# Two DMAs where there was one for the stacked heads, and a denser order for normalising the next batch, in an attention stage between two expert layers

## The reference

```python
x = x + 0.5 * ffn(layernorm(x))        # top 2 of 8 experts, silu(gate) * up, down
x = x + attn(layernorm(x))             # 16 heads of 16
x = x + 0.5 * ffn(layernorm(x))

# attn
q = x @ W_q ; k = x @ W_k ; v = x @ W_v
latent = (k + v) @ W_down_kv           # 64 wide
k_rec, v_rec = latent @ W_up_k, latent @ W_up_v
scores = (q k_rec^T) / 16 * exp(-0.01 |i - j|)
out = softmax(scores) @ v_rec @ W_o
```

## Time and profile before

| what | value |
|---|---|
| median of three runs | 6439.68 us (6439.29 to 6446.07) |
| the profiled execution | 6439.29 us, its span 6437.5 us |
| attention stage in the span | about 1110 to 5320 us |
| one batch of it, from batch 3 on | about 252.9 us (64 steps) |
| mean granted TensorE clock over the span | 0.946 |

### The profile page before, as it was taken

How to read it: one execution, slowest core, us unless ns; L and a number is a source line. 1 busy time by engine, 2 the same in 40 slices (tenths; PEclk the granted TensorE clock), 3 DMA queues, 4 the chain that set the end, 5 groups by cost and what they waited for, 6 DMA issues and landing times.

```text
span 6437.5 us, 111424 instructions
## 1 busy us (share of the span) xinstructions
PE 5494.3 (85%) x35660; PEld 3210.9 (50%) x35660; DVE 4607.0 (72%) x14349; ACT 3194.0 (50%) x4421; POOL 2850.2 (44%) x2837
## 2 busy tenths in 40 slices
PE   4459998379999999999999999999999993999771
PEld 4448887134444444444444444444444442888561
DVE  6556565268888888888888888888888883555453
ACT  1124443146666665666666666656666662444220
POOL 5630000653655646646546556466474332000445
PEclk9999999589999999999999999999999996999885
DMA  4423333344544544544445444445444432333556
GB/s 150 149 98 105 105 105 110 98 95 86 123 100 105 121 103 111 122 100 118 112 97 124 99 107 120 103 109 122 99 112 99 87 66 89 100 105 109 167 187 188
DMA packets 531513, 725.27 MB, mean 113 GB/s; under 512 B 79491, under 2 KB 447237, under 8 KB 530949
## 3 DMA queue, kind: packets, MB, share of 16 engines
q1 hardware_dynamic: 481796, 583.86, 37.7%
q0 software_dynamic: 49152, 134.28, 6.5%
HBM read 424.53 MB, written 293.34 MB: 112 GB/s over the span
## 4 chain that ended last, share of the span: by engine, by line
PE 59%; POOL 16%; DVE 10%; issue 9%; another core or an unknown queue 2%; ACT 2%; DMA 2%; SPq 1%; POOLq 0%; ACTq 0%; DVEq 0%
PE psum L1205 12%; PE psum L1055 11%; PE psum L374 11%; PE psum L1064 7%; PE psum L391 5%; DVE at_mx L1317 4%; PE psum L1068 2%; POOL at_xT L1440 2%; POOL at_XR L1471 2%; POOL at_Sd L1531 2%; PE psum L1112 2%; PE psum L363 2%; PE psum L382 2%; POOL at_XR L1449 2%
## 5 line engine op out<-in xcount | busy, mean ns | idle before, releaser
L1265 ACT ACTIVATE at_P<-psum 128x1024 f32<-128x1024 f32 x2048 | 2034.7, 1023 | 1317.0 <-PE psum L1068 1252.6
L1317 DVE TENSOR_REDUCE at_mx<-psum 128x4 f32<-128x512 f32 x3584 | 2229.1, 682 | 432.2 <-PE psum L1055 380.0
L1055 PE MATMUL psum<-at_kst,at_qst 96*128 96x128 bf16 (+3 forms) x7168 | 1611.2, 295 | 186.3 <-DVE at_mx L1317 124.8
L1064 PE MATMUL psum<-at_qst,at_kst 99*128 99x512 bf16 (+3 forms) x5120 | 1467.6, 320 | 7.2 <-ACT at_P L1265 7.1
L1055 PEld LDWEIGHTS psum<-at_kst,at_qst 96*128 96x128 bf16 x7168 | 598.5, 98 | 1491.5 <-DVE at_mx L1317 609.0
L1205 PE MATMUL psum<-at_P,at_V 128*17 128x512 f32 x8192 | 1099.3, 608 | 0.0
L1531 POOL TENSOR_TENSOR at_Sd<-at_Sd,at_m 128x1024 f32<-128x1024 f32 x256 | 484.4, 1898 | 943.5 <-DVE at_m L1326 941.7
L669 POOL DMA_INDIRECT m2Y<-ys,m2yi x256 | 243.5, 951 | 797.3 <-issue 626.3
L1068 PE MATMUL psum<-at_ident,at_Sd 128*128 128x128 f32 x2048 | 565.3, 276 | 0.0
L1064 PEld LDWEIGHTS psum<-at_qst,at_kst 99*128 99x128 bf16 x5120 | 493.7, 99 | 143.1 <-ACT at_P L1265 18.2
L1312 DVE CUSTOM_DVE_ANT_0 at_Sd<-psum,at_Dm 128x128 f32<-128x128 f32 x2048 | 443.2, 286 | 87.1 <-PE psum L1055 87.0
(11 more groups left out here) (246 smaller groups left out, 7950.6 us busy)
## 6 DMA issues: line engine op xcount, KB each, us to landing
parts<-at_pt SPq DMA_DIRECT2D x768, 128.0 KB
at_qst<-parts SPq DMA_DIRECT2D x768, 128.0 KB
at_kst<-parts SPq DMA_DIRECT2D x128, 384.0 KB
m2X<-xs SPq DMA_DIRECT2D x272, 128.0 KB, 2.0
ys<-m2X SPq DMA_DIRECT2D x272, 128.0 KB
m1X<-xs SPq DMA_DIRECT2D x264, 128.0 KB, 2.0
ys<-m1X SPq DMA_DIRECT2D x264, 128.0 KB
at_kst<-parts SPq DMA_DIRECT2D x128, 256.0 KB
```

The lines of the kernel that those rows point to most:

```text
L1055: ins = e.matmul(bank[z % 3][:, col - 512 * u:col - 512 * u + ln], self.qst[0:96, s, side, 128 * t:128 * t + 128], self.kst[0:96, s, 1 - s ...
L1064: e.matmul(slot[a % 2][:, q0:q0 + ln], self.kst[0:99, s, side, 128 * kb:128 * kb + 128], self.qst[0:99, s, 1 - side, q0:q0 + ln], start=Tr ...
L1265: e.activation(self.P[:, i % NP, :], slot[a % 2], ACT.Exp).then_inc(self.taken.sem, 1)
L1317: e.tensor_reduce(self.mx[:, p % 2, hh, 8 * o + 4 * u:8 * o + 4 * u + 4], of, op=ALU.max, axis=AX.X).then_inc(self.s_read.sem, 1)
```

## The change

The stack of a pair is issued head by head, so it takes 18 DMAs instead of 9, of half the size each; the semaphore counts follow (144 becomes 288). In `gather_order` the statistics are done two to a slot, `var` shares the slot of the last two, and the eight `center` are done in two slots instead of four, with no empty slot behind them. In `unit_order` the `send` of a projection comes right in the slot after its second `rest`, instead of in the next projection's.

```diff
-        self.stacked = sig.ring("a_stacked", [144 * n for n in shares_of(NPAIR, NS)])
+        self.stacked = sig.ring("a_stacked", [288 * n for n in shares_of(NPAIR, NS)])
...
         for t in range(8):
-            yield from (("stats", b, t), None)
+            yield ("stats", b, t)
+            if t % 2 and t < 7:
+                yield None
         yield from (("var", b), None, ("newton", b), None)
         for t in range(8):
             yield ("center", b, t)
-            if t % 2:
+            if t == 3:
                 yield None
         yield None
...
         for i in range(8):
-            yield from (("project", b, i), None, ("cast", b, i, 0), None, ("rest", b, i, 0))
-            if i:
-                yield ("send", b, i - 1)
-            yield from (None, None, ("cast", b, i, 1), None, ("rest", b, i, 1), None)
+            yield from (("project", b, i), None, ("cast", b, i, 0), None, ("rest", b, i, 0), None, None,
+                        ("cast", b, i, 1), None, ("rest", b, i, 1), None, ("send", b, i))
         for t2 in range(4):
-            yield ("values", b, t2)
-            if t2 == 2:
-                yield ("send", b, 7)
-            yield None
+            yield from (("values", b, t2), None)
...
-                    w.wait_ge(*self.stacked[s].at(144 * len(range(s, 8 * (b - 1), NS))))
+                    w.wait_ge(*self.stacked[s].at(288 * len(range(s, 8 * (b - 1), NS))))
...
-                h = 2 * (p % 8)
-                qd, kd = self.qst[:, 2 * s:2 * s + 2], self.kst[:, 2 * s:2 * s + 2]
-                for c, (r0, r1) in enumerate(((0, 3), (3, 5), (5, 6))):
-                    for r in range(r0, r1):
-                        e.dma_start(qd[16 * r:16 * r + 16], src[0, h:h + 2, c].rearrange("h d v t -> d h v t")).then_inc(done, 16)
-                for r0, n in ((0, 3), (48, 2), (80, 1)):
-                    e.dma_start(kd[r0:r0 + 16 * n], src[1, h:h + 2, 0:n].rearrange("h c d v t -> (c d) h v t")).then_inc(done, 16)
+                for hh in range(2):
+                    h = 2 * (p % 8) + hh
+                    qd, kd = self.qst[:, 2 * s + hh], self.kst[:, 2 * s + hh]
+                    for c, (r0, r1) in enumerate(((0, 3), (3, 5), (5, 6))):
+                        for r in range(r0, r1):
+                            e.dma_start(qd[16 * r:16 * r + 16], src[0, h, c]).then_inc(done, 16)
+                    e.dma_start(kd[0:48], src[1, h].rearrange("c d v t -> (c d) v t")).then_inc(done, 16)
+                    e.dma_start(kd[48:80], src[1, h, 0:2].rearrange("c d v t -> (c d) v t")).then_inc(done, 16)
+                    e.dma_start(kd[80:96], src[1, h, 0]).then_inc(done, 16)
...
-            w.wait_ge(*self.stacked[n // 2 % NS].at(144 * (n // 2 // NS + 1)))
+            w.wait_ge(*self.stacked[n // 2 % NS].at(288 * (n // 2 // NS + 1)))
```

## The result

The changed kernel takes 6646.19 us (median of 4 runs, 6639.33 to 6653.74) against 6442.88 us (4 runs) for the kernel before: a ratio of 1.0314, 95% interval 1.0297 to 1.0332. The forecast was slower, +150 us to 6589 with a range up to 6645. The measured change is +203, and the time lies 1 us above that range: the sign and the main cause hold, and one term is missing.

A forecast was written before the change was run, and what follows sets the result against it. PE and DVE were taken to run in lockstep over three banks, PE a little ahead. Denser gather 140, batches 0 to 2 5 + 3, first stack 2, earlier send 0: 150 on 6439.3, so 6589 us; 8-in-10 range 6495 to 6645.

The forecast's parts named there:

- the stop at the turn: PE at a batch's first turn transpose: stands 8.9 us for GpSimd's last center, against 0.7 before, 8.2 more.
- part 1: Denser gather order in the attention stage: 10.8 us per batch, 140 us over 13 batches.
- GpSimd's chain: GpSimd's own work from newton to the last center in a batch: 22.5 us.
- The clock term: PE at half clock behind the stop at the turn: +3.0 us for each batch.
- The crowding of DVE: Stats moved into steps 410 to 413, where DVE is the slower engine: +0.8 us a batch.
- The bounds between the halves: Denser gather order: bounds of 7 to 13 us a batch for the whole, no figure for stats or center alone.
- Batches 0 to 2: Gather of the first batches: nothing in batch 0, +5 us in batch 1, +3 in batch 2.
- the first stacks: At the start, where PE waits for the first stack issued as 18 DMAs: +2 us (0 to 4).
- The stacks: 18 DMAs for a stack on SP: transfers stay slower than 8.6 us of issues; steady stage pays nothing.
- the rival of late stacks: Fixed cost per DMA uses up the stacks' margin, so scores wait: about 6700 us, chance 0.09.
- The earlier send: Send two steps sooner on SP: may put msend off some 4 us, with at least 9 to spare: 0.
- part 4: The send issued two steps sooner on SP's queue: 0 us (0 to +15).

The follow-up runs named there:

- e2: Kernel before with only the denser gather order (stats in pairs, center in two slots, no empty slot behind): 6372.5 us, ratio 1.0223.
- e5: Changed kernel with 60 identity transposes on PE ahead of its wait at the first turn of batches 3 to 15: 6396.9 us, ratio 1.0258.
- e7: Kernel before with only the stats two to a slot and var with the last two: 6271.0 us, ratio 1.0059.
- e6: Kernel before with only the eight center in two slots and no empty slot behind them: 6376.1 us, ratio 1.0225.
- e1: Kernel before with only the stack issued head by head, 18 DMAs for 9: 6232.4 us, ratio 0.9996.
- e3: Kernel before with only the send moved right behind its second rest: 6299.0 us, ratio 1.0101.
- e8: Kernel before with the send one slot behind the next project, so behind msend on SP's queue: 6241.1 us, ratio 1.0005.
- e11: Kernel before with one more empty slot ahead of the turns and the stats begun one slot later: 6375.0 us, ratio 0.9893.

## Why the prediction was right in its direction and short by 53 us

- **Slower, by the stop at the turn** (part 1): right, nearly to the figure. GpSimd's chain 22.5 us forecast, 22.3 measured; the stop 8.9 and 8.05; the gain in a batch 10.8 and 10.4 (e2); the part as a whole 140 and 137. The clock term of 3.0 us is borne out by e5 with some 3 to 4, in the changed kernel. That the sum came out so near is in part luck, as the next point shows.
- **The crowding of DVE** (+0.8 a batch): too small. e7 shows 2.1, since the short stops behind DVE also pull the clock down. In the sum of part 1 this was made up by a stop 0.8 us shorter and by what came back elsewhere: in e2 PE's busy time grows by only 1.6 us a batch for crowding and stop together, and in e7 by 2.0 for the crowding alone.
- **The bounds between the halves**: the sum did not say what each half would do, and e6 shows that center in two slots is enough for all of it.
- **Batches 0 to 2** (+8) and the first stacks (+2): 3.4 us measured up to batch 3.
- **The stacks** (0 in the steady stage): right, and the rival of late stacks wrong (e1). The reason given, that the DMA engines are slower than 18 issues, was wrong: with smaller DMAs they got faster and had room while the issues went on. That the end came out nearly the same (11.3 us against 10.7) was luck.
- **The earlier send** (part 4: 0, at most +15): this is the step that failed. It said that msend may be put off by some 4 us and has at least 9 to spare. It is put off by 9.2, as the six issues (3.65 us) and the wait for a late rest (5.5 us) both count, and then its halves lie 2.8 us further apart (4.2 for 1.4): 12.0 in all. Of the 9.0 us between the last issue and PE in the kernel before, some 1.3 are the landing (3028.10 to 3029.41 in the changed kernel), so an estimate of what was to spare is 7.7, and the 4.3 that are missing are about PE's stop of 4.03. The 6.4 us at most of the earlier trace rows were waits of sends that came three steps after their rest; in the changed order the send comes one step after it and SP meets the rest itself, which on GpSimd stands behind r_center and gathers. It happens once in a batch, not twice. Its price is 4.6 us a batch and 64 in all (e3), and e8 shows that it hangs on the place ahead of msend alone.

With that term the sum would have been 150 + 64 = 214, beside 203.

## What to carry to other kernels

When an item is moved in a list that every engine follows in order, add up what the producing engine still has ahead of it up to the consumer's new place, and compare that with the time of the steps between; here 22 us of work met four steps of 15 us in all. Do the same for a DMA queue: a transfer that waits for a late producer delays whatever stands behind it by the wait, by its issues and, as it seems here, by its bytes, so small urgent transfers belong ahead of large ones that nobody awaits. A stop of TensorE can cost more than its length where the clock falls behind it (e5, 37 us), though not in every sum (e3 paid the 64 us of the wait alone). Look for room in the other direction too: two empty slots more made this kernel 1.1% faster (e11), probably by removing short stops of PE in crowded steps.

## What the runs showed of the hardware that was not expected

Splitting a stack's DMAs by head, with the same bytes and the same pieces of 4 KB, made the DMA engines quicker: SP's queue takes 31.2% of the engines' time in e1 and 37.7% in the kernel before (37.9% in e3, which has the old stack beside the same 6235 us) for the same 583.9 MB, and behind one stack the DMA share adds up to 6.1 us of engine time in e1 where it is 9.9 us before (the sums of six windows of 2 us each). Of the windows of 2 us behind that stack the fullest in e1 carries 207 GB/s at a share of 0.76, and in the kernel before 168 GB/s at 1.06. The Trainium skill ("DMA: Bandwidth & Descriptors", Bandwidth) says that efficiency grows with the size of a DMA, by figures for DMAs that GpSimd issues; these runs, with SP issuing, go the other way for 64 KB against 128 KB with two pieces of 4 KB in each partition. Why was not tried.
